# One decoder layer on one core: first layer norm folded into the second, router taken apart, all stages placed anew

## The chip, the cores and the metric

One Trainium2 chip, of which one core is used. Everything is in 32-bit floats. The metric is the time of one execution on the device in microseconds (us); lower is better. TensorE is PE in the profile, VectorE is DVE, ScalarE is ACT, GpSimd is POOL and SyncE, which here only issues DMAs, is SP.

## The reference, cut to what is computed

A decoder layer over 128 sequences of 64 tokens with 128 features each, three blocks with a layer norm (no gain, no bias) behind each sum:

```python
x = layernorm(x + mamba(x))                     # LN1
x = layernorm(x + retention(x, ctx, ctx))       # LN2
x = layernorm(x + moe(x))                       # LN3

# mamba: 256 inner channels, 16 states, 4 taps
x_b, z = split(x @ W_in)
xc = silu(conv4(x_b) + conv_b)
delta_raw, B, C = split(xc @ W_xproj)           # 8, 16 and 16 columns
delta = softplus(delta_raw @ W_dt + b_dt)
h = exp(delta * A) * h + delta * B * xc         # over time, for each channel and state
y = (sum_s h * C + D * xc) * silu(z)
out = y @ W_out

# retention: q of x, k and v of ctx, positions rotated (xpos), no softmax
out = ((q @ k.T) * decay_mask) @ v              # within a sequence

# moe: 16 experts of 64, the 2 best by logits, plus one shared expert of 128
logits = x @ router_w.T + bias
two scores of the best two, softmax over the two -> combine (tokens x 16)
out = sum_e combine_e * (silu(x @ gate_e) * (x @ up_e)) @ down_e + shared(x)
```

## The kernel before, in words

**Tiling.** The 8192 tokens are cut into 17 chunks: 15 of 512 tokens (8 whole sequences) with one of 256 at either end. A chunk is two halves ("subs") of 256 tokens; the scan of a sub takes 8 steps, each for `PAIR` = 2 of the 16 states. That makes 256 steps in the run, and a chunk of 512 tokens has 16. Channels lie on the 128 partitions, 256 inner channels as two halves side by side, so that each scan is 128 x 512.

**One step.** ACT makes the decays of the step by four exps of 128 x 252 (`decay`, L680, seven buffers). DVE multiplies delta*xc with the broadcast B of two states (`drive_bank` from `dx_bank` and `bc_all`, L720, two drives) and runs two scans (`state`, L822). POOL multiplies the states with C (`read`, L873, 128 x 1024, two buffers for states and reads). PE adds the results up over the states by eight transposes into `y_bank` (L287). B and C reach all partitions by DMA: SP stores `proj` to DRAM and loads it back in broadcast, four states a load (`bc_all`, L982, three buffers).

**The rest of a chunk** is done between the steps of others: input transpose, convolution (its first half as four matmuls on PE, its second half as three multiply-adds `conv` on DVE, L690), `xc` (ACT, L636 and L642), `proj`, `delta`; `y_gated` (DVE, L730), its transpose, the output projection `out_mm`; LN1; retention (`k_rot`, `q_rot` and their kin on POOL, L889 to L906); LN2; the router (DVE, L785 to L815, with an exp of ACT, L669, in the middle); then nine tiles of the FFN: a gate matmul, `silu` (ACT, L656), an up matmul, their product (DVE, L837; called `hid` for the shared expert and `gu` for the eight pairs of experts), the product with the experts' weights of the tokens (POOL `hid`, L916) and the down matmul. The weights of the tokens are broadcast by DMA too: `comb` is transposed (`combT`), stored (L1000) and loaded row by row (`comb_all`, L1009, three buffers).

**Layer norms.** All weights that feed a norm are centred once at the start (L742 to L758), so that the mean is zero and only a variance is wanted. A norm is: ACT squares four blocks of 128 x 128 with their sums (`square`, L522 to L528), POOL forms `var_eps` (L848) and `rstd` by a power (L852), ACT multiplies each block with it (`normalise`, L530 to L534). For LN1 PE then transposes the normalised rows `x1` and ACT copies the result as `x1T`.

**What sets the order of the work.** Each engine runs one program written out by a loop over `slot`, two slots a step, in which an `if` for each stage asks `chunk_at(slot, where, last)` whether this is the stage's slot; `where` is its place relative to the chunk, `last` that of the last chunk. Within a slot the order is that of the code. On DVE an even slot holds the two drives, an odd one the two scans, and everything else stands ahead of both or behind both. The nine tiles of the FFN have the places `FFN_AT`, and the exps of a sub are spread over seven slots (`decays_at`). Engines meet by semaphores; each waits in its own order, so whatever stands behind a waiting instruction waits too. Three PSUM banks are shared by all the matmuls that are not sums over a chunk: `take` hands out the one whose `slot` is lowest. The places around the change, as the code has them:

```python
EXP_AT = [10, 27]
FFN_AT = [69, 70, 72, 76, 78, 84, 88, 90, 91]
LAST_FFN_AT = [67, 68, 69, 71, 71, 74, 75, 77, 78]
if k % 2 == 0 and 0 <= (j := k // 2) < STEPS:       # two drives
if k % 2 == 1 and 0 <= (j := k // 2) < STEPS:       # two scans
```

## Time and profile before

| | |
|---|---|
| median of 3 runs | 1212.84 us (1212.56 to 1213.9) |
| profiled execution | 1216.39 us, its span 1214.6 us |
| mean granted clock of PE | 0.967 |
| first drive | 29.85 us |
| end of the last scan | 1137.6 us |
| DMA | 194.55 MB, 160 GB/s |

The span is cut in three: a head of 30 us until DVE begins the scans, 1108 us of steps, and a tail of 77 us in which the retention of the last chunk and the FFN of the last two are finished. The page gives for each engine its busy time; the windows view gives it for a stretch; the timeline lists instructions with their start, their duration and, in brackets, how long the engine had been idle and what released it. An instruction's duration overlaps with the next one's start where the two are independent, so a cost is read from start to start. In this profile the scans are called TENSOR_TENSOR_SCAN; in the lists of orders below they are SCALAR_TENSOR_TENSOR `state<-decay,drive_bank`.

### The profile page before, as it was taken

The page shows a single profiled execution, that of the slowest core. Times are in us where ns is not written, and L with a number is a line of the kernel's source. Part 1 is how long each engine was busy: PE and PEld are TensorE (multiplying, and loading weights), DVE is VectorE, ACT ScalarE, POOL GpSimd, SP SyncE. Part 2 cuts the span into 40 slices and gives each one's busy share as a digit, 9 for nine tenths or more (in the row PEclk, how much of TensorE's full clock was granted, in tenths as well). Part 3 has the DMA queues.
Part 4 walks back from the last instruction along what each step waited for, and adds up shares of the span by engine and source line. Part 5 has one row for each costly group of instructions (what it writes and reads, how often), then busy time and mean ns, then how long its engine had stood idle before and what let it go on. Part 6 is the DMA issues. An engine that isn't in the chain of part 4 may idle for free.

```text
span 1214.6 us, 18948 instructions
## 1 busy us (share of the span) xinstructions
PE 1080.0 (89%) x6049; PEld 766.0 (63%) x6049; DVE 1093.3 (90%) x1598; ACT 997.8 (82%) x2288; POOL 989.8 (81%) x623
## 2 busy tenths in 40 slices
PE   5677888989999898999989898998989899988897
PEld 2455666666666766666666666666666667666565
DVE  2899999999999999999999999999999999999523
ACT  5677888989888898988889898988889898888343
POOL 0587797979988897998888799888979888898844
PEclk9687999999999999999999999999999999999999
DMA  6344454545464454546455444645444465454221
GB/s 181 141 164 154 142 174 150 187 141 182 158 202 158 159 183 143 188 150 209 150 169 173 159 173 153 206 160 173 159 172 161 157 204 165 159 179 158 70 80 58
DMA packets 84116, 194.55 MB, mean 160 GB/s; under 512 B 17288, under 2 KB 47936, under 8 KB 67632
## 3 DMA queue, kind: packets, MB, share of 16 engines
q1 hardware_dynamic: 84016, 193.33, 47.3%
q8 instruction: 48, 0.79, 0.3%
q14 instruction: 52, 0.43, 0.1%
HBM read 179.14 MB, written 5.77 MB: 152 GB/s over the span
## 4 chain that ended last, share of the span: by engine, by line
ACT 34%; DVE 26%; PE 24%; issue 11%; POOL 3%; DMA 0%; SPq 0%; DVEq 0%; POOLq 0%; ACTq 0%
ACT decay L680 15%; PE bank L283 14%; DVE state L822 14%; DVE drive_bank L720 6%; PE y_bank L287 6%; ACT L680 4%; ACT silu L656 2%; PE down_bank L283 2%; PE bank L287 2%; ACT L636 1%; ACT L648 1%; ACT L656 1%; POOL hid L916 1%; ACT x_rows L526 1%; POOL read L873 1%
## 5 line engine op out<-in xcount | busy, mean ns | idle before, releaser
L873 POOL TENSOR_TENSOR read<-state,bc_all 128x1024 f32<-128x1024 f32 x256 | 605.4, 2365 | 162.4 <-DVE state L822 139.0
L822 DVE TENSOR_TENSOR_SCAN state<-decay,drive_bank 128x512 f32<-128x512 f32 x512 | 593.9, 1200 | 0.0
L680 ACT ACTIVATE decay<-delta,a_neg 128x252 f32<-128x252 f32 x1024 | 420.4, 494 | 0.8
L720 DVE TENSOR_TENSOR drive_bank<-dx_bank,bc_all 128x512 f32<-128x512 f32 x512 | 327.3, 685 | 0.3 <-DVE state L822 0.3
L287 PE MATMUL y_bank<-ident,read 128*128 128x128 f32 x2048 | 285.7, 287 | 40.4 <-POOL read L873 40.3
L287 PEld LDWEIGHTS y_bank<-ident,read 128*128 128x128 f32 x2048 | 246.2, 148 | 90.6 <-POOL read L873 57.6
L916 POOL TENSOR_TENSOR hid<-gu,comb_all 128x512 f32<-128x512 f32 (+1 forms) x136 | 165.0, 1213 | 20.1 <-DVE gu L837 16.6
L283 PE MATMUL down_bank<-down_w,hid 128*128 128x128 f32 x1024 | 140.9, 280 | 15.1 <-POOL hid L916 12.6
L656 ACT ACTIVATE silu<-bank 128x512 f32<-128x512 f32 (+1 forms) x153 | 87.3, 571 | 81.4 <-PE bank L283 79.6
L283 PEld LDWEIGHTS down_bank<-down_w,hid 128*128 128x128 f32 x1024 | 127.0, 191 | 38.0 <-POOL hid L916 28.6
L837 DVE TENSOR_TENSOR gu<-silu,bank 128x512 f32<-128x512 f32 (+1 forms) x136 | 86.8, 638 | 56.7 <-PE bank L283 30.0
L283 PE MATMUL bank<-x2T,gate_w 128*128 128x512 f32 (+1 forms) x272 | 132.9, 570 | 1.6 <-DVE conv L690 0.7
L283 PE MATMUL bank<-x2T,up_w 128*128 128x512 f32 (+1 forms) x272 | 132.7, 569 | 0.3 <-ACT silu L656 0.2
L283 PEld LDWEIGHTS bank<-x2T,up_w 128*128 128x128 f32 x272 | 51.2, 190 | 60.2 <-issue 52.8
L680 ACT ACT_TABLE_LOAD x63 | 80.8, 1283 | 1.1
L283 PE MATMUL bank<-xT,w_tap 128*128 128x512 f32 (+7 forms) x136 | 59.4, 582 | 0.0
L533 ACT ACTIVATE x_rows<-bank,rstd 128x128 f32<-128x128 f32 x128 | 36.9, 375 | 26.7 <-POOL rstd L852 26.7
L656 ACT ACT_TABLE_LOAD x45 | 57.7, 1283 | 0.8
L883 POOL TENSOR_TENSOR dx<-xc,delta 128x512 f32<-128x512 f32 x32 | 40.9, 1278 | 18.5 <-ACT delta L664 18.5
L852 POOL TENSOR_TENSOR rstd<-var_eps,minus_half 128x4 f32<-128x4 f32 (+1 forms) x51 | 49.7, 974 | 4.3
L283 PE MATMUL bank<-x2T,shared_w 128*128 128x512 f32 (+1 forms) x68 | 37.2, 638 | 16.9 <-ACT gate_z L648 11.4
L283 PEld LDWEIGHTS bank<-x2T,gate_w 128*128 128x128 f32 x272 | 42.8, 191 | 11.7 <-issue 8.0
(126 smaller groups left out, 1496.3 us busy)
## 6 DMA issues: line engine op xcount, KB each, us to landing
bc_all<-bc_dram SPq DMA_DIRECT2D x128, 1024.0 KB, 4.9
comb_all<-comb_dram SPq DMA_DIRECT2D x240, 128.0 KB, 4.5
x_in<-in_x_dram SPq DMA_DIRECT2D x15, 256.0 KB, 6.0
ctx_in<-in_ctx_dram SPq DMA_DIRECT2D x15, 256.0 KB, 5.2
k_pair<-k_pair SPq DMA_DIRECT2D x30, 128.0 KB, 2.1
q_pair<-q_pair SPq DMA_DIRECT2D x30, 128.0 KB, 2.0
out_dram<-y_out SPq DMA_DIRECT2D x15, 256.0 KB, 5.6
comb_all<-comb_dram SPq DMA_DIRECT2D x32, 64.0 KB, 2.7
```

The source lines that it names most:

```text
L283: return e.matmul(out, lhsT, rhs, start=start, stop=stop, skip_group_check=True)
L287: return e.matmul(out, in_, identity[0:n, 0:n], is_transpose=True, start=start, stop=stop, skip_group_check=True)
L533: done = e.activation(out[:, q, :], blocks(bank)[:, q, :], ACT.Copy, scale=rstd[i][:, q:q + 1])
L656: e.activation(silu[total % 2][:, 0:width(c)], bank_of["gate", c, index][:, 0:width(c)], ACT.Silu, scale=1.0).then_inc(S["silu"], 1)
L680: done = e.activation(seqs(decay_t[j % DECAYS][:, i, h, :])[:, :, 1:T], seqs(delta[c % 2][:, h, sub * SUB:(sub + 1) * SUB])[:, :, 1:T], AC ...
L720: e.tensor_tensor(drive_bank[:, n, :, :], dx_bank[:, :, :], bc_all[group % BC_BUFS][:, 0, PAIR * i + n, :].unsqueeze(1).to_broadcast([P, H ...
L822: e.tensor_tensor_scan(one(state_t[j % STATE_BUFS], n), one(decay_t[j % DECAYS], n), one(drive_bank, n), 0.0, ALU.mult, ALU.add).then_inc( ...
L837: e.tensor_tensor(target[:, 0:width(c)], silu[total % 2][:, 0:width(c)], bank_of["up", c, index][:, 0:width(c)], ALU.mult).then_inc(S["gu" ...
L852: e.tensor_tensor(rstd[i][:, 0:n], var_eps[i][:, 0:n], minus_half[:, 0:n], ALU.pow).then_inc(RSTD[i], 1)
L873: e.tensor_tensor(read_t[j % READS][:, :, :, :], state_t[j % STATE_BUFS][:, :, :, :], bc_all[group % BC_BUFS][:, 1, PAIR * i:PAIR * (i + 1 ...
L883: e.tensor_tensor(dx[sub][:, :, :], xc[c % 2][:, :, cols], delta[c % 2][:, :, cols], ALU.mult).then_inc(S["dx"], 1)
L916: e.tensor_tensor(hid[index % 3][:, 0:width(c)], gu[index % 2][:, 0:width(c)], comb_all[use % COMBS][:, 0:width(c)], ALU.mult).then_inc(S[ ...
```

## The change

**LN1 is folded into LN2.** Everything between LN1 and LN2 is linear in x1 (q is, the retention is, the sum is), so the scale of LN1 is a common factor of each token that LN2 takes out again; only the epsilon of LN2 has to be multiplied by LN1's variance (plus its epsilon) instead. `out_mm` now makes x1 directly in transposed form and without its scale, by three matmuls of up to 512 columns. The first, with `center`, stands ahead of the wait for y. ACT copies it as `x1T` and squares it into `r1_sq`; PE sums the squares over the features against a column of epsilons (`r1_var_mm`), ACT copies the 128 x 4 result, and POOL adds it in LN2's `var_eps`. Gone are LN1's squares and normalisation on ACT, its `var_eps` and `rstd` on POOL and its transposes on PE.

```diff
-                if (c := chunk_at(slot, 36, 33)) is not None:
-                    bank = take(("out", c), slot, 4.5)
+                for c in due(tick, "out_mm"):
+                    bank = take(("out", c), tick, 3)
+                    w.wait_ge(S["centered"], 1)
+                    mm(bank.t[:, 0:width(c)], center[:, :], xT[c % 3][:, 0:width(c)], stop=False)
                     w.wait_ge(S["yT"], subs_after(c))
-                    w.wait_ge(S["centered"], 1)
-                    for q in range(blocks_of(c)):
-                        cols = slice(q * P, (q + 1) * P)
-                        mm(bank.t[:, cols], xT[c % 3][:, cols], center[:, :], stop=False)
-                        for h in range(HALVES):
-                            done = mm(bank.t[:, cols], y_gatedT[:, h, cols], w_out[:, h, :], start=False,
-                                      stop=h == HALVES - 1)
+                    for h in range(HALVES):
+                        done = mm(bank.t[:, 0:width(c)], w_out[:, h, :], y_gatedT[:, h, 0:width(c)], start=False,
+                                  stop=h == HALVES - 1)
...
+                for c in due(tick, "r1_var_mm"):
...
+                    for q in range(blocks_of(c)):
+                        done = mm(bank.t[:, 2 * q:2 * q + 2], r1_sq[:, q * P:(q + 1) * P], eps_col[:, :])
...
-                    square(bank_of["out", c][:, :], x1, LN1, c)
-                if (c := chunk_at(slot, 38, 35)) is not None:
-                    normalise(bank_of["out", c][:, :], x1, LN1, c)
...
+                    copy(x1T[:, 0:width(c)], bank_of["out", c][:, 0:width(c)]).then_inc(S["x1T"], 1)
+                    w.wait_ge(S["r1_var_mm"], at(c - 1))
+                    e.activation(r1_sq[:, 0:width(c)], bank_of["out", c][:, 0:width(c)], ACT.Square, scale=D ** -0.5).then_inc(
+                        S["r1_sq"], 1)
...
+                if i == LN2:
+                    w.wait_ge(S["r1_var"], at(c))
+                    e.tensor_tensor(var_eps[i][:, 0:n], squares[i][:, 0:n], r1_var[:, 0:n], ALU.add).then_inc(VAR_EPS[i], 1)
```

**The router** has 17 operations for 19: the softmax over two is made by a tanh in place of exp, sum, reciprocal and product, the two scores are `0.5*tanh + 0.5` and `-0.5*tanh + 0.5`, and the two weighted ranks are one product of 128 x 128. Each operation has its own place.

**The grid.** A step has four ticks in place of two slots, on DVE one for each drive and scan, so that something may stand between any two. All places are a table of (place, place in the last chunk) in ticks, read by `due(tick, name)`; gate and up matmuls, silu, product, POOL's product, down matmul and comb load have a list of their own each, and every one of a chunk's 16 decays a tick.

```diff
+TICKS, SUM_AFTER = 4, 2
+SUB_TICKS = TICKS * SUB_STEPS
...
+AT = {
...
+    "top_tanh": [(131, 119)],
...
+    "k_rot": [(73, 88)],
...
+    "q_rot": [(86, 67)],
...
+    "silu": [
+        (139, 136), (140, 139), (144, 139), (152, 159), (157, 175), (167, 192), (177, 213), (177, 226), (178, 228)],
+    "gu": [
+        (142, 144), (144, 144), (149, 149), (157, 162), (160, 176), (171, 191), (179, 191), (184, 226), (188, 232)],
...
+    "route": [
+        (127, 108), (130, 109), (131, 110), (132, 111), (133, 112), (133, 113), (134, 114), (134, 115), (134, 116),
+        (134, 117), (134, 118), (134, 119), (134, 120), (135, 120), (135, 122), (136, 122), (136, 123)],
+}
+EXP_AT = [-9, -8, -2, -2, -2, 1, 4, 16, 22, 24, 26, 33, 36, 37, 38, 52]
...
+                j, part = divmod(tick, TICKS)
+                if 0 <= j < STEPS and part < PAIR:
...
+                    e.tensor_tensor(drive_bank[:, part, :, :], dx_bank[:, :, :],
...
+                if 0 <= j < STEPS and part >= PAIR:
+                    n = part - PAIR
...
+                for c, op in due(tick, "route"):
                     n = blocks_of(c)
...
+                    elif op == 12:
+                        done = e.tensor_tensor(soft[:, 0, 0:n], top[:, 0, 0:n], top[:, 1, 0:n], ALU.subtract)
+                    elif op in (13, 14):
+                        w.wait_ge(S["top_tanh"], at(c))
+                        done = e.tensor_scalar(soft[:, op - 11, 0:n], soft[:, 1, 0:n], 0.5 if op == 13 else -0.5, 0.5, ALU.mult, ALU.add)
+                    elif op == 15:
+                        w.wait_ge(S["combT_mm"], at(c - 1))
+                        done = e.tensor_tensor(rank[:, :, 0:n, :], comb[:, 0:2, 0:n, :],
+                                               soft[:, 2:4, 0:n].unsqueeze(3).to_broadcast([P, 2, n, EXPERTS]), ALU.mult)
+                    else:
+                        done = e.tensor_tensor(comb[:, 2, 0:n, :], rank[:, 0, 0:n, :], rank[:, 1, 0:n, :], ALU.add)
...
-                if slot % GROUP == 0 and 0 <= (group := slot // GROUP + 2) < ALL_SUBS * GROUPS:
+                if tick % (GROUP_STEPS * TICKS) == 0 and 0 <= (group := tick // (GROUP_STEPS * TICKS) + 2) < ALL_SUBS * GROUPS:
```

In the last chunk, the head and the tail all places are new too. In the head ACT's copies of the transposed weights (`w_qkv`, `shared_w`, `w_router`) stood behind the exps of decay 3 to 6, 16 instructions, and now stand behind decay 3's four.

**The order on DVE at a chunk's router.** This is the second router of the run. Before:

```order
L730 TENSOR_TENSOR y_gated<-gate_z,y_bank 128x512 [waits s_gate_z,s_y]
L785 TENSOR_TENSOR logits<-bank1,router_bias 128x64 [waits s_router_mm]
L771 TENSOR_REDUCE top<-logits 128x4 [waits s_comb,s_router]
L773 TENSOR_TENSOR rank<-logits,top 128x64 [waits s_router]
L775 TENSOR_TENSOR rank<-rank,expert_back 128x64 [waits s_router]
L777 TENSOR_REDUCE top_at<-rank 128x4 [waits s_router]
L779 TENSOR_TENSOR comb<-expert_back,top_at 128x64 [waits s_router]
L690 SCALAR_TENSOR_TENSOR masked<-comb,logits 128x64 [waits s_router]
L771 TENSOR_REDUCE top<-masked 128x4 [waits s_router]
```

and in the changed kernel:

```order
L799 SCALAR_TENSOR_TENSOR state1<-decay4,drive_bank 128x512 [waits s_drive]
L848 TENSOR_TENSOR logits<-bank0,router_bias 128x64 [waits s_comb,s_router_mm]
L791 TENSOR_TENSOR drive_bank<-dx_bank,bc_all2 128x512 [waits s_bc_load2,s_dx_bank,s_state]
L791 TENSOR_TENSOR drive_bank<-dx_bank,bc_all2 128x512 [waits s_state]
L799 SCALAR_TENSOR_TENSOR state0<-decay5,drive_bank 128x512 [waits s_read,s_decay,s_drive]
L852 TENSOR_REDUCE top<-logits 128x4 [waits s_router]
L799 SCALAR_TENSOR_TENSOR state0<-decay5,drive_bank 128x512 [waits s_drive]
L855 TENSOR_TENSOR rank<-logits,top 128x64 [waits s_router]
L791 TENSOR_TENSOR drive_bank<-dx_bank,bc_all2 128x512 [waits s_state]
L857 TENSOR_TENSOR rank<-rank,expert_back 128x64 [waits s_router]
L791 TENSOR_TENSOR drive_bank<-dx_bank,bc_all2 128x512 [waits s_state]
L806 TENSOR_TENSOR y_gated<-gate_z,y_bank 128x512 [waits s_gate_z,s_y]
```

The router was one block between a drive pair's `y_gated` and the scans. Now its first operations stand one by one behind a drive or a scan and start a step earlier. The further ones: two behind `y_gated`, seven behind the next scan, two behind the other scan, two behind the next drive.

**The order on ACT at the second half of `xc`**, in the middle of a chunk's FFN. Before:

```order
L520 ACTIVATE dx_bank<-dx1 128x512 [waits s_drive,s_dx]
L636 ACT_TABLE_LOAD [waits s_y]
L636 ACTIVATE xc_0<-bank0,conv_b 128x512 [waits s_tap_mm]
L642 ACTIVATE xc_0<-conv 128x512 [waits s_conv_tap]
L656 ACTIVATE silu1<-bank2 128x512 [waits s_gu,s_gate_mm]
L680 ACT_TABLE_LOAD
L680 ACTIVATE decay2<-delta1,a_neg 128x4x63 [waits s_state]
```

and in the changed kernel:

```order
L594 ACTIVATE dx_bank<-dx1 128x512 [waits s_drive,s_dx]
L709 ACT_TABLE_LOAD [waits s_y]
L709 ACTIVATE xc_0<-bank0,conv_b 128x512 [waits s_tap_mm]
L725 ACTIVATE silu1<-bank2 128x512 [waits s_gu,s_gate_mm]
L715 ACTIVATE xc_0<-conv 128x512 [waits s_conv_tap]
L749 ACT_TABLE_LOAD
L749 ACTIVATE decay2<-delta1,a_neg 128x4x63 [waits s_state]
```

The silu of an FFN tile (`silu1`) now stands between the two halves of `xc` instead of behind both. On DVE the product `gu` that reads it stood behind the scans of the step and ahead of the next two drives; it now stands between these two drives.

**The order on SP**, the DMA issues around a router's result. Before:

```order
L982 DMA bc_all1<-bc_dram1 128x2048 [waits s_read]
L1017 DMA ctx_in1<-in_ctx_1024_dram 128x4x128 [waits s_ctxT_mm]
L1000 DMA comb_dram1<-combT 16x512 [waits s_combT]
L982 DMA bc_all2<-bc_dram1 128x2048 [waits s_read]
L1009 DMA comb_all2<-comb_dram1 64x512 [waits s_hid,s_comb_store1]
L1009 DMA comb_all2<-comb_dram1 64x512
L1009 DMA comb_all0<-comb_dram1 64x512 [waits s_hid]
```

and in the changed kernel:

```order
L1040 DMA k_pair<-k_pair 64x512
L1033 DMA bc_all1<-bc_dram1 128x2048 [waits s_read]
L1051 DMA comb_dram1<-combT 16x512 [waits s_combT]
L1059 DMA comb_all2<-comb_dram1 64x512 [waits s_hid,s_comb_store1]
L1059 DMA comb_all2<-comb_dram1 64x512
L1059 DMA comb_all0<-comb_dram1 64x512 [waits s_hid]
L1059 DMA comb_all0<-comb_dram1 64x512
L1033 DMA bc_all2<-bc_dram1 128x2048 [waits s_read]
```

The broadcast load of `bc_all2` stood between the store of `combT` and the first loads of `comb_all`; now it stands behind the store and four of these loads.

## Rows read from the trace of the kernel before

**Rows 1.** The page's section 1: busy time, share of the span, instructions of each engine
```profile
PE 1080.0 (89%) x6049; PEld 766.0 (63%) x6049; DVE 1093.3 (90%) x1598; ACT 997.8 (82%) x2288; POOL 989.8 (81%) x623
```

**Rows 2.** Windows, chunk by chunk: length, busy time and count per engine, clock, DMA
```profile
443.33:514.50 71.17, 66.37 (x375) 47.18 (x374) 67.64 (x99) 61.67 (x142) 61.51 (x38) 0.98 0.49 168
514.50:584.12 69.62, 64.93 (x375) 45.43 (x374) 67.42 (x98) 61.66 (x142) 61.55 (x38) 1.00 0.52 172
...
sum 352.17, PE 328.49 PEld 232.30 DVE 337.74 ACT 308.33 POOL 307.67; mean PE 65.70 PEld 46.46 DVE 67.55 ACT 61.67 POOL 61.53
```

**Rows 3.** Timeline of DVE, one router block: start, duration, operation, [idle before]
```profile
544.82 0.22 DVE L785 TENSOR_TENSOR logits<-bank,router_bias 128x64 f32<-128x64 f32 x1
545.08 0.22 DVE L771 TENSOR_REDUCE top<-logits 128x4 f32<-128x64 f32 x1
...
548.44 0.17 DVE L804 TENSOR_SCALAR soft<-soft 128x4 f32<-128x4 f32 x1 [0.27 <-ACT soft L669]
...
549.45 0.23 DVE L815 TENSOR_TENSOR comb<-rank 128x64 f32<-128x64 f32 x1
549.59 2.32 DVE L822 TENSOR_TENSOR_SCAN state<-decay,drive_bank 128x512 f32<-128x512 f32 x2
```

**Rows 4.** Timeline of DVE, the steps behind that block
```profile
551.83 1.27 DVE L720 TENSOR_TENSOR drive_bank<-dx_bank,bc_all 128x512 f32<-128x512 f32 x2
553.01 2.32 DVE L822 TENSOR_TENSOR_SCAN state<-decay,drive_bank 128x512 f32<-128x512 f32 x2
555.25 1.27 DVE L720 TENSOR_TENSOR drive_bank<-dx_bank,bc_all 128x512 f32<-128x512 f32 x2
...
567.59 1.27 DVE L720 TENSOR_TENSOR drive_bank<-dx_bank,bc_all 128x512 f32<-128x512 f32 x2
```

**Rows 5.** Waits of DVE over the whole run: us in total, times, longest
```profile
DVE gu L837 <- ACT silu L656: 25.5, 23, 1.8
...
DVE hid L837 <- issue: 2.5, 13, 0.2
```

**Rows 6.** Timeline of DVE at the longer silu wait
```profile
578.30 0.69 DVE L837 TENSOR_TENSOR gu<-silu,bank 128x512 f32<-128x512 f32 x1 [1.15 <-ACT silu L656]
```

**Rows 7.** Timeline of ACT ahead of that wait
```profile
577.16 0.62 ACT L642 ACTIVATE xc<-conv 128x512 f32<-128x512 f32 x1
577.68 0.59 ACT L656 ACTIVATE silu<-bank 128x512 f32<-128x512 f32 x1
```

**Rows 8.** Windows of 2 us where the clock falls (columns as in rows 2)
```profile
452.00:454.00 2.00, 2.00 (x12) 2.00 (x11) 2.00 (x3) 1.28 (x9) 0.85 (x1) 0.50 0.95 264
```

**Rows 9.** Timeline of DVE behind that stretch
```profile
457.52 0.69 DVE L837 TENSOR_TENSOR gu<-silu,bank 128x512 f32<-128x512 f32 x1 [1.02 <-ACT silu L656]
```

**Rows 10.** Group of ACT: count | busy us, mean ns | idle before
```profile
L533 ACT ACTIVATE x_rows<-bank,rstd 128x128 f32<-128x128 f32 x128 | 36.9, 375 | 26.7 <-POOL rstd L852 26.7
```

**Rows 11.** Group of POOL, columns as in rows 10
```profile
L852 POOL TENSOR_TENSOR rstd<-var_eps,minus_half 128x4 f32<-128x4 f32 (+1 forms) x51 | 49.7, 974 | 4.3
```

**Rows 12.** Timeline of DVE in the head
```profile
39.07 0.29 DVE L751 TENSOR_REDUCE row_sum<-w_qkv 128x1 f32<-128x128 f32 x1 [4.51 <-ACT shared_w L520]
```

**Rows 13.** Timeline of ACT in the head
```profile
31.85 6.44 ACT L680 ACTIVATE decay<-delta,a_neg 128x252 f32<-128x252 f32 x16
...
38.56 0.47 ACT L520 ACTIVATE shared_w<-bank 128x384 f32<-128x384 f32 x1
```

**Rows 14.** Timeline of PE in the head
```profile
34.33 0.28 PE L287 MATMUL bank<-ident,router_rows 16*128 16x16 f32 x1
```

**Rows 15.** Timeline of ACT in the tail
```profile
1160.59 0.28 ACT L526 ACTIVATE x_rows<-bank 128x128 f32<-128x128 f32 x1 [0.20 <-PE bank L283]
...
1164.12 0.38 ACT L520 ACTIVATE x1T<-bank 128x256 f32<-128x256 f32 x1 [0.31 <-PE bank L287]
```

**Rows 16.** Timeline of SP's DMA issues
```profile
554.37 0.32 SPq L982 DMA_DIRECT2D bc_all<-bc_dram  x1
```

**Rows 17.** The page's section 6: DMA issues, count, KB each, us to landing
```profile
bc_all<-bc_dram SPq DMA_DIRECT2D x128, 1024.0 KB, 4.9
```

More of the change, by code:

```diff
@@ new lines, in decoder_layer @@
+        DUE = {name: {} for name in AT}
+        for name, places in AT.items():
+            for n, (normal, last) in enumerate(places):
+                due_of(name, n, normal, last)
+        EXP_DUE = {}
+        for j in range(STEPS):
+            half, n = divmod(j, SUB_STEPS)
+            virtual, sub = divmod(half + 1, SUBS)
+            step = SUB_STEPS * sub + n
+            place = SUB_TICKS * (SUBS * virtual - 1) + (EXP_AT[step] if virtual < CHUNKS - 1 else LAST_EXP_AT[step])
+            EXP_DUE.setdefault(place, []).append(j)
@@ L267, in decoder_layer, with due @@
+        ticks = [tick for places in (*DUE.values(), EXP_DUE) for tick in places]
+        FIRST_TICK, LAST_TICK = min(ticks), max(*ticks, TICKS * (STEPS + SUM_AFTER)) + 1
+        def due(tick, name):
+            return DUE[name].get(tick, ())
         block = ctx.enter_context(nc.Block())
@@ L301, in _ @@
                     bank.free = (S["xT"], at(c))
-                if (c := chunk_at(slot, -19, -18)) is not None:
-                    bank = take(("xb", c, 0), slot, 1.5)
+                for c in due(tick, "tap_mm"):
+                    bank = take(("xb", c, 0), tick, 3)
                     w.wait_ge(S["xT"], at(c))
@@ L364, in _ @@
                     bank.free = (S["ctxT"], at(c))
-                if (c := chunk_at(slot, 35, 35)) is not None:
-                    bank = take(("k", c), slot, 1)
+                for c in due(tick, "k_mm"):
+                    bank = take(("k", c), tick, 2)
                     w.wait_ge(S["ctxT"], at(c))
@@ L370, in _ @@
                     bank.free = (S["k_copy"], at(c))
-                if (c := chunk_at(slot, 36, 35)) is not None:
-                    bank = take(("v", c), slot, 1)
+                for c in due(tick, "v_mm"):
+                    bank = take(("v", c), tick, 2)
                     w.wait_ge(S["ctxT"], at(c))
@@ L413, in _ @@
+                for c in due(tick, "q_mm"):
+                    bank = take(("q", c), tick, 2)
                     w.wait_ge(S["x1T"], at(c))
@@ L443, in _ @@
                     bank.free = (S["x2T"], at(c))
-                if (c := chunk_at(slot, 63, 56)) is not None:
-                    bank = take(("router", c), slot, 1.5)
+                for c in due(tick, "router_mm"):
+                    bank = take(("router", c), tick, 3)
                     w.wait_ge(S["x2T"], at(c))
@@ L536, in _ @@
             w.wait_ge(S["first_consts"], 16 * 6)
-            for slot in range(FIRST, LAST):
-                if (c := chunk_at(slot, -21, -23)) is not None:
+            for tick in range(FIRST_TICK, LAST_TICK):
+                for c in due(tick, "xT"):
                     w.wait_ge(S["xT_mm"], at(c))
@@ L657, in _ @@
                                  scale=1.0).then_inc(S["silu"], 1)
-                if (c := chunk_at(slot, -9, -9)) is not None:
+                for c in due(tick, "delta"):
                     for h in range(HALVES):
@@ L828, in _ @@
+                    done.then_inc(S["comb" if op == 16 else "router"], 1)
+                for c, index in due(tick, "gu"):
                     total = TILES * c + index
@@ L890, in _ @@
                                     ALU.mult).then_inc(S["k_rot"], 1)
-                if (c := chunk_at(slot, 41, 43)) is not None:
+                for c in due(tick, "k"):
                     w.wait_ge(S["k_rot"], at(c))
@@ L899, in _ @@
                                     ALU.mult).then_inc(S["q_rot"], 1)
-                if (c := chunk_at(slot, 44, 36)) is not None:
+                for c in due(tick, "q"):
                     w.wait_ge(S["q_rot"], at(c))
@@ L984, in _ @@
                                     BC_LOAD[group % BC_BUFS], 16)
-                if (c := chunk_at(slot, 29, 38)) is not None:
+                for c in due(tick, "k_swap"):
                     w.wait_ge(S["k_copy"], at(c))
```

569 lines of the change are left out of this document (288 added, 281 removed).

## The prediction

> **What bounds the kernel now.** I read three views in this order: the busy line of the page, the windows chunk by chunk, and DVE's timeline inside one chunk. The busy line puts DVE and PE side by side, 1093.3 and 1080.0 us [rows 1], so it does not name the bound. The windows do [rows 2]: from one router block to the next, a chunk of 512 tokens takes 71.17 or 69.62 us, 70.43 in the mean of five (352.17 / 5), and DVE is busy for 67.55 of it. ACT has 61.67 and POOL 61.53. PE shows 65.70, but its records overlap and their ends are modelled, so I take it as having a few us of room. DVE is the bound, and what it does not work is waits of its own. Its timeline shows the price of one step [rows 4]: two drives 1.18 us (551.83 to 553.01) and two scans 2.24 (to 555.25), 3.42 together, 16 times a chunk = 54.7 us, which the change leaves alone. Some 15.7 us a chunk are router, `gu` and `hid` products, gates, taps and waits. There the change acts.
>
> **Term 1, the router.** Before, 19 small DVE operations stand in one block behind `y_gated`: 544.82 to 549.59 [rows 3] = 4.77 us, among them 0.27 us of waiting for ACT's exp. Neighbours that depend on each other start 0.26 us apart (544.82, 545.08) though one lasts 0.22. A follower that depends on nothing in the block starts earlier: the last comb starts at 549.45 and the scan behind it at 549.59, so this comb costs 0.14. After, 17 operations are spread over ten ticks. Eight small ones have a drive, scan or gate ahead and can take the 0.14 price (counting the 128x128 product at 0.2, my estimate by its size between the 0.23 of 128x64 and the 0.69 of 128x512 [rows 6]), the other nine follow one another at 0.26 or a little less: 7 x 0.14 + 0.2 + 9 x 0.25 = 3.43. The exp wait goes too, since a whole scan stands between the subtraction and the first use of ACT's tanh. Saving 4.77 - 3.43 = 1.34 us, at least 4.77 - 17 x 0.256 = 0.42 if place gives nothing, at most 4.77 - 17 x 0.14 = 2.4. I take 1.34 because both prices are rows of this very block. 14 routers lie in the pipeline: **-18.8 us** (5.9 to 34). The Trainium skill (Perfetto Trace Analysis, "Optimizing Scalar/DVE Operations") gives each DVE instruction on SBUF a fixed overhead of about 60 ns, counts the second half of its profiled time as covered by the next one, and advises fewer, larger operations. By it a small operation has one price wherever it stands, only the two that are left out and the exp wait count, and the sum would be rival A's. The trace does not agree: its price is 0.14 or 0.26 in one block, by what the operation has ahead of it.
>
> **Term 2, DVE's waits for silu.** DVE waits 25.5 us in 23 places for ACT's silu [rows 5]. 13 of them are 1.15 us, one a chunk [rows 6]: ACT, with no pause, copies xc's second half at 577.16 and only then does the silu at 577.68 [rows 7]. After, silu stands ahead of that copy (0.5 us earlier) and `gu` stands behind one more drive (0.6 later): 1.1 of 1.15 should go. 13 x 1.1 = **-14.3 us**, between 0 (ACT is later for another reason) and -15. Eight more are 1.02 us [rows 9] (13 x 1.15 + 8 x 1.02 = 23.1 of the 25.5; the other two lie at the run's ends). They follow a stretch in which PE's granted clock is 0.50 [rows 8], so that the gate matmul, and with it the silu, is late. Nothing in the change reaches this directly: 0 taken, -8.2 if the places happen to cover it. The 0.19 waits ahead of `hid` (2.5 us in 13 [rows 5]) and the one wide pair of taps that is taken apart are under 0.2 us a chunk each: 0 taken, -2.5 at most.
>
> **Term 3, the folded layer norm.** For each chunk ACT loses four squares with their accumulator reads and four normalising copies, and gains one 512-wide square (like a 0.59 silu [rows 7]) and a tiny copy. Whole-run, half of x_rows' 36.9 us of normalising [rows 10] goes, and half of its squares with it. POOL loses one of three rstd, 974 ns each [rows 11], and the `var_eps` before it. PE swaps twelve narrow matmuls for three wide ones, drops four transposes and adds four of two columns, about even. None of the three engines bounds a chunk [rows 2], so in the pipeline I cost this at nothing. DVE's cover is what hides it: if DVE were gone, ACT's 61.7 would be next, 6 us below what I forecast for a chunk. On POOL a read may now stand behind k_rot or q_rot, which were behind reads before; the scan two steps later waits for it, so up to one 2.4 us product fits without a DVE wait.
>
> **Term 4, the head.** DVE stands 4.51 us for ACT's copy of the shared weights [rows 12], because ACT does 16 decay pieces from 31.85 ahead of it and reaches the copy at 38.56 [rows 13]. PE has the transposed weights ready at 34.61 (34.33 + 0.28) [rows 14]. After, only four pieces are ahead (1.6 us), so that PE's transposes set the copy. The wait shrinks to some 0.3 us: **-4.2 us**, between 0 (the decays put off are then missed by a scan) and -4.5.
>
> **Term 5, the tail.** Behind the last scan ACT's x_rows square at 1160.59 leads by rstd, normalise and PE's transposes to the x1T copy at 1164.12 [rows 15]; after, this is one copy: **-3.5 us**. Bounds: 0, since the last chunk's FFN queues behind the one before it on PE, and -10 with the new places.
>
> **The sum.** -18.8 - 14.3 - 4.2 - 3.5 = -40.8. The profiled execution took 1216.39 us (span 1214.6), 3.55 over the median of 1212.84. 1216.39 - 40.8 = 1175.6; less 3.55, **1172.0 us**. A chunk should take 70.43 - 1.34 - 1.0 = 68.1 us.
>
> **Rivals.**
> A, *place gives nothing*: small operations cost 0.256 everywhere. Router -5.9 in place of -18.8: 1184.9 us. For it: 16 of the 17 still carry a wait on the one before. Against: the 0.14 row.
> B, *the waits stay*: ACT's and PE's order moves the silu wait elsewhere and the tail gives nothing, -23.0 left: 1189.8 us. For it: all stages were moved at once on three shared PSUM banks. Against: ACT has 2 us a chunk more room.
> C, *all waits go*: 8.2 + 2.5 + 0.7 more, and 6.5 more in the tail, -58.7: 1154.1 us. For it: a grid twice as fine can reach them; against: the clock's falls are not the grid's.
> D, *slower, by the bc load*: before, SP issues bc_all at 554.37 ahead of the comb loads [rows 16], it takes 4.9 us to land [rows 17], and the drive at 567.59 [rows 4] is the first to need it: 8.3 us of slack. After, this load stands behind the comb store, which waits for the router's result, and four comb loads; I estimate 5.5 us later (the landing of the store, the four issues, and a comb that is ready a tick later), 2.8 of slack. Each us beyond costs 14 us in the run, every drive and scan being queued behind. It decides from 2.9 us (40.8 / 14) over the slack on; at 4 us, -40.8 + 56 = +15.2: 1228.0 us. Against: comb would have to be over 5.7 us later than I estimate, and DVE's router starts five ticks earlier.
> E, *nothing net*: smaller new waits of some 2.9 us a chunk of any engine eat the gain: about 1213.
>
> **How the numbers follow.** Forecast 0.49, A 0.14, B 0.14, C 0.12, D 0.08, E 0.03. About 0.2%, 2.4 us, is what a measurement here can tell from no change. Faster: the first four, 0.89; same 0.03; slower 0.08. The forecast's own range is 1165 to 1180. The whole range takes in C, A and B with a few us: 1153 to 1195, and leaves out D, E and what lies below C.
>
> **What would show it.** Router: between two steps that hold a router operation, 0.14 us more than 3.42 for each single one; a chunk at 68.1. Silu: no 1.15 row ahead of `gu`, but 1.02 rows still behind stretches at clock 0.50. Head: DVE's wait for shared_w near 0.3. POOL and ACT about 60 and 59 us a chunk. The prediction is wrong if a chunk stays above 70 us or if DVE waits for a DMA of bc_all, for a read, or for decays each chunk.

## The result, and the profile after

The changed kernel takes 1254.85 us (median of 4 runs, 1254.38 to 1255.52) against 1212.71 us: a ratio of 1.035, 95% interval 1.033 to 1.036. It is 42 us slower where 41 us less was forecast.

The page of the changed kernel, its busy line, which answers to [rows 1]:

```profile
span 1252.6 us, 18269 instructions
...
PE 1072.2 (86%) x5831; PEld 752.8 (60%) x5831; DVE 1160.4 (93%) x1564; ACT 975.3 (78%) x2128; POOL 972.0 (78%) x590
```

PE, ACT and POOL have less to do, as meant. DVE has 34 instructions fewer and is busy 67.1 us longer. Its idle time (span less busy) fell from 121.3 to 92.2 us. So the span's 38.0 us are +67.1 of busy DVE and -29.1 of waits: in their sum the waits went as forecast or a little better, and the loss lies inside instructions that count as busy.

The windows chunk by chunk, from router to router as in [rows 2]:

```profile
413.74:486.32 72.58, 65.01 (x362) 45.20 (x361) 71.86 (x96) 60.48 (x132) 60.47 (x35) 0.98 0.50 165
...
558.90:632.82 73.92, 64.69 (x363) 45.25 (x361) 71.99 (x96) 60.48 (x132) 60.43 (x35) 0.98 0.46 162
...
sum 365.72, PE 324.33 PEld 226.71 DVE 359.56 ACT 302.35 POOL 302.25; mean PE 64.87 PEld 45.34 DVE 71.91 ACT 60.47 POOL 60.45
```

A chunk takes 73.14 us (before 70.43, forecast 68.1), and DVE is busy for 71.91 of them (67.55). The groups of DVE (count | busy us, mean ns | idle before) say which instructions:

```profile
L868 DVE TENSOR_SCALAR soft<-soft 128x4 f32<-128x4 f32 (+1 forms) x34 | 38.3, 1128 | 1.5 <-ACT soft L738 1.0
...
L857 DVE TENSOR_TENSOR rank<-rank,expert_back 128x64 f32<-128x64 f32 (+1 forms) x34 | 33.4, 983 | 0.7
L871 DVE TENSOR_TENSOR rank<-comb,soft 128x128 f32<-128x128 f32 (+1 forms) x17 | 30.2, 1776 | 0.1
...
L861 DVE TENSOR_TENSOR comb<-expert_back,top_at 128x64 f32<-128x64 f32 (+1 forms) x34 | 7.5, 221 | 1.2
L859 DVE TENSOR_REDUCE top_at<-rank 128x4 f32<-128x64 f32 (+1 forms) x34 | 7.1, 210 | 0.7
```

Three kinds of router operation are some four to seven times as long as work of their size; the others stay at 0.16 to 0.22 us. One chunk's timeline on DVE shows them one by one:

```profile
557.67 0.20 DVE L852 TENSOR_REDUCE top<-logits 128x4 f32<-128x64 f32 x1
...
559.62 1.88 DVE L857 TENSOR_TENSOR rank<-rank,expert_back 128x64 f32<-128x64 f32 x1
...
564.88 0.23 DVE L857 TENSOR_TENSOR rank<-rank,expert_back 128x64 f32<-128x64 f32 x1
...
566.87 2.55 DVE L868 TENSOR_SCALAR soft<-soft 128x4 f32<-128x4 f32 x2
...
569.93 1.90 DVE L871 TENSOR_TENSOR rank<-comb,soft 128x128 f32<-128x128 f32 x1
```

And the same stretch on POOL:

```profile
556.13 2.38 POOL L926 TENSOR_TENSOR read<-state,bc_all 128x1024 f32<-128x1024 f32 x1
559.07 2.35 POOL L926 TENSOR_TENSOR read<-state,bc_all 128x1024 f32<-128x1024 f32 x1 [0.55 <-DVE state L799]
...
567.03 2.36 POOL L926 TENSOR_TENSOR read<-state,bc_all 128x1024 f32<-128x1024 f32 x1 [4.24 <-DVE state L799]
569.34 2.34 POOL L941 TENSOR_TENSOR k_pair<-k_pair,xpos 128x1024 f32<-128x1024 f32 x1
```

Each long operation ends with a POOL instruction: 559.62 + 1.88 = 561.50 and the read ends at 561.42; 566.87 + 2.55 = 569.42 and the read ends at 569.39; 569.93 + 1.90 = 571.83 and k_rot ends at 571.68. The second `rank<-rank,expert_back`, of the same shape, runs at 564.88, when POOL is idle, in 0.23. What stands still all have two operands in SBUF (or are a tensor_scalar from SBUF to SBUF); the reduce at 557.67 has one and takes 0.20 in the middle of the read of 556.13. Drives, scans and gates have their second operand in PSUM (`dx_bank`, `drive_bank`, `y_bank`) and never show it.

The Trainium skill says it outright (SBUF — State Buffer, "Who interferes with whom"): a DVE instruction with two SBUF inputs contends with a GpSimd instruction that reads SBUF, whichever comes first holds the shared port for its whole length and the other fully blocks; a tensor_scalar can contend too, by a mode that takes both of DVE's ports, and a tensor_reduce never does. For these three the trace agrees, with 1.7, 2.2 and 1.6 us a chunk more than the same work takes in the run e1 below. The prediction should have weighed this page, and did not.

The hint had been in the trace of before: the first rank operation of the router took 0.33 us instead of 0.22, because it began 0.25 us before a read's end. The rest of the block ran while POOL did two operations of 128x4 (`var_eps`, `rstd`) and then, waiting for the scans behind the block, was idle.

### The profile page after: what moved, and what is told of

Its sections match the earlier page's. It is cut to its first block, busy times and chain, and to the rows that moved or that the text cites. A ratio compares the mean times of both kernels' runs of the same rounds, so it can differ in the third digit from the quotient of the medians.

```text
span 1252.6 us, 18269 instructions
## 1 busy us (share of the span) xinstructions
PE 1072.2 (86%) x5831; PEld 752.8 (60%) x5831; DVE 1160.4 (93%) x1564; ACT 975.3 (78%) x2128; POOL 972.0 (78%) x590
## 4 chain that ended last, share of the span: by engine, by line
PE 32%; POOL 17%; ACT 17%; DVE 16%; issue 16%; DMA 1%; SPq 1%; POOLq 0%; ACTq 0%; DVEq 0%
PE bank L361 18%; POOL read L926 11%; DVE state L799 7%; ACT decay L749 7%; PE y_bank L370 6%; PE down_bank L361 5%; POOL hid L967 3%; DVE drive_bank L791 3%; PE bank L370 3%; DVE rank L871 2%; ACT L749 2%; ACT L709 2%; ACT silu L725 2%; POOL ret L958 1%; POOL dx L935 1%
## 5 line engine op out<-in xcount | busy, mean ns | idle before, releaser
L799 DVE TENSOR_TENSOR_SCAN state<-decay,drive_bank 128x512 f32<-128x512 f32 x512 | 602.2, 1206 | 0.0
L791 DVE TENSOR_TENSOR drive_bank<-dx_bank,bc_all 128x512 f32<-128x512 f32 x512 | 336.6, 685 | 0.0
L370 PE MATMUL y_bank<-ident,read 128*128 128x128 f32 x2048 | 274.6, 280 | 45.2 <-POOL read L926 45.2
L370 PEld LDWEIGHTS y_bank<-ident,read 128*128 128x128 f32 x2048 | 238.3, 144 | 93.6 <-POOL read L926 54.9
L725 ACT ACTIVATE silu<-bank 128x512 f32<-128x512 f32 (+1 forms) x153 | 87.6, 574 | 96.6 <-PE bank L361 96.2
L361 PE MATMUL bank<-x2T,up_w 128*128 128x512 f32 (+1 forms) x272 | 133.7, 574 | 10.2 <-ACT proj L594 6.8
L361 PE MATMUL down_bank<-down_w,hid 128*128 128x128 f32 x1024 | 135.3, 277 | 0.7 <-POOL hid L967 0.7
L887 DVE TENSOR_TENSOR gu<-silu,bank 128x512 f32<-128x512 f32 (+1 forms) x136 | 88.2, 649 | 34.8 <-PE bank L361 20.7
L361 PEld LDWEIGHTS bank<-x2T,up_w 128*128 128x128 f32 x272 | 46.9, 190 | 52.6 <-issue 31.4
L935 POOL TENSOR_TENSOR dx<-xc,delta 128x512 f32<-128x512 f32 x32 | 41.0, 1281 | 18.8 <-ACT delta L733 18.8
L361 PE MATMUL bank<-xc,w_xproj 128*40 128x512 f32 (+1 forms) x68 | 34.4, 634 | 24.1 <-ACT xc L715 23.6
L594 ACT ACTIVATE combT<-bank 16x512 f32<-16x512 f32 (+1 forms) x17 | 9.5, 561 | 55.2 <-PE bank L370 55.2
L370 PE MATMUL bank<-ident,y_gated 128*128 128x128 f32 x128 | 22.4, 303 | 32.3 <-DVE y_gated L806 32.3
```

What stands on the lines that cost most here:

```text
L361: return e.matmul(out, lhsT, rhs, start=start, stop=stop, skip_group_check=True)
L370: return e.matmul(out, in_, identity[0:n, 0:n], is_transpose=True, start=start, stop=stop, skip_group_check=True)
L725: e.activation(silu[total % 2][:, 0:width(c)], bank_of["gate", c, index][:, 0:width(c)], ACT.Silu, scale=1.0).then_inc(S["silu"], 1)
L791: e.tensor_tensor(drive_bank[:, part, :, :], dx_bank[:, :, :], bc_all[group % BC_BUFS][:, 0, PAIR * i + part, :].unsqueeze(1).to_broadcast ...
L799: e.tensor_tensor_scan(one(state_t[j % STATE_BUFS], n), one(decay_t[j % DECAYS], n), one(drive_bank, n), 0.0, ALU.mult, ALU.add).then_inc( ...
L887: e.tensor_tensor(target[:, 0:width(c)], silu[total % 2][:, 0:width(c)], bank_of["up", c, index][:, 0:width(c)], ALU.mult).then_inc(S["gu" ...
```

## The experiments

Theory L: the lock just described. Rival P: small operations are dear on DVE behind large ones, or in their new forms. Rival W: waits in another place. In this table idle is span less busy of DVE, from each profiled run. The kernel before, run beside each group of experiments, gave 1214.5 us (e1 to e3), 1214.3 (e4 to e7) and 1215.9 (e8 to e11), so that 2 or 3 us between two groups mean nothing.

| run | time, us | span | DVE busy | DVE idle |
|---|---|---|---|---|
| before | 1212.7 | 1214.6 | 1093.3 | 121.3 |
| changed | 1254.9 | 1252.6 | 1160.4 | 92.2 |
| e1, router one block again | 1180.8 | 1179.0 | 1084.6 | 94.4 |
| e2, k_rot a step later | 1225.0 | 1223.3 | 1135.7 | 87.6 |
| e10, early rank product into the block | 1247.6 | 1245.4 | 1138.3 | 107.1 |
| e11, tensor_scalars into the block | 1267.1 | 1264.7 | 1161.9 | 102.8 |
| e4, e1 with three edits | 1180.4 | 1180.3 | 1083.2 | 97.1 |
| e5, e1 with a norm's work put back | 1192.5 | 1190.0 | 1084.1 | 105.9 |
| e7, e1 with all 17 in the block | 1206.0 | 1203.1 | 1087.8 | 115.3 |
| e8, e1 with the tanh early | 1175.1 | 1171.5 | 1084.3 | 87.2 |
| e9, e8 with operation 2 alone | 1174.4 | 1171.2 | 1082.9 | 88.3 |
| e3, before with POOL reading beside the router | 1236.3 | 1233.8 | 1116.2 | 117.6 |
| e3, before with memsets beside it | 1214.6 | 1212.4 | 1094.4 | 118.0 |
| e6, before with the router ahead of the drives | 1284.1 | 1281.8 | 1120.5 | 161.3 |

**e1: only the places of the router undone.** Of the changed kernel's table, 13 numbers:

```diff
-        (127, 108), (130, 109), (131, 110), (132, 111), (133, 112), (133, 113), (134, 114), (134, 115), (134, 116),
-        (134, 117), (134, 118), (134, 119), (134, 120), (135, 120), (135, 122), (136, 122), (136, 123)],
+        (127, 108), (130, 109), (134, 110), (134, 111), (134, 112), (134, 113), (134, 114), (134, 115), (134, 116),
+        (134, 117), (134, 118), (134, 119), (134, 120), (134, 120), (134, 122), (134, 122), (134, 123)],
```

> The changed kernel with operations 2 to 16 of the router together again at one place, between a step's two scans, where POOL has finished its read; operations 0 and 1, all other places, the folded norm and the 17 operations stay as changed. Theory L (a DVE operation that reads two SBUF operands, or a tensor_scalar in SBUF, stands still while POOL runs one that reads SBUF): no router operation over 0.4 us, DVE busy about 5 us a chunk less, 1254.9 - 14 x 5 = about 1185 us. Rival P (small operations are dear behind a drive or scan for a reason of DVE's own, or are dear because of the new forms, the 128x128 product and the tensor_scalars): the 128x128 product stays near 1.9 us and the tensor_scalars near 1.1, time above 1220. Rival W (other new waits are the loss): 1240 or more.

Measured 1180.81 us, 74.0 less than changed and 0.9725 (0.9711 to 0.974) of before. Groups of DVE in this run:

```profile
L857 DVE TENSOR_TENSOR rank<-rank,expert_back 128x64 f32<-128x64 f32 (+1 forms) x34 | 8.6, 252 | 1.2
...
L871 DVE TENSOR_TENSOR rank<-comb,soft 128x128 f32<-128x128 f32 (+1 forms) x17 | 5.9, 348 | 0.6
L868 DVE TENSOR_SCALAR soft<-soft 128x4 f32<-128x4 f32 (+1 forms) x34 | 5.8, 170 | 6.7 <-ACT soft L738 6.1
```

The same instructions, forms and operands, 75.8 us less busy. So new forms and other new waits are out as the cause, and the fold, the new places of everything else and the 17 operations together are a gain of 32 us (34 against the runs of before beside it). "No router operation over 0.4 us" holds in 16 of the 17 routers; in the last one, in the tail, two take 1.25 and 1.31 us beside POOL's `hid` products, as they do in the changed kernel. A chunk takes 68.29 us in this run (`logits` at 321.68 and 389.97), where the prediction had 68.1.

**e3: the lock brought into the kernel before.** In the program of POOL, behind the read of the router's step, where it had been idle for 5 us:

```diff
+                if (c := chunk_at(slot, 65, 56)) is not None:
+                    w.wait_ge(S["extra"], at(c - 1, 1, 2))
+                    e.tensor_tensor(extra[:, :], extra_in[:, :], extra_in[:, :], ALU.mult).then_inc(S["extra"], 1)
+                    w.wait_ge(S["extra"], at(c, 0, 2))
+                    e.tensor_tensor(extra[:, :], extra_in[:, :], extra_in[:, :], ALU.mult).then_inc(S["extra"], 1)
```

and in the second run `e.memset(extra[:, :], 1.0)` twice instead.

> The kernel before with two additional POOL multiplications of 128x512 (about 1.2 us each, SBUF to SBUF, result unused) in each chunk behind the read ahead of the router block, where POOL had been idle for 5 us. Theory L: they overlap with the router block and its two-operand operations wait for them; the block takes 1 to 2.4 us more, 14 x 1.7 = 24 us more, 1235 us (1225 to 1246), and some rank operations show 1 us or more. Rival P: POOL was idle, nothing changes, 1213 us.

> As the run with the additional multiplications, but with two memsets of 128x512 in their place, which read nothing. Theory L in the form that only POOL's reads of SBUF stand in the way of a second operand: no change for the rank operations; at most the four tiny tensor_scalar-like ones could meet them, 1213 us within 2. If POOL's work of any kind blocks DVE: as much more as with the multiplications, in proportion to the memsets' own time.

Measured 1236.29 us (ratio 1.018, 1.017 to 1.020) and 1214.58 (1.0005, 0.9996 to 1.0015; the runs of before beside them had 1214.46). With the multiplications DVE is busy for 22.9 us more than in before. Timeline of DVE with the multiplications, and of POOL:

```profile
551.57 0.97 DVE L777 TENSOR_TENSOR rank<-rank,expert_back 128x64 f32<-128x64 f32 x1
552.57 0.22 DVE L779 TENSOR_REDUCE top_at<-rank 128x4 f32<-128x64 f32 x1
552.83 0.83 DVE L781 TENSOR_TENSOR comb<-expert_back,top_at 128x64 f32<-128x64 f32 x1
```

```profile
551.41 1.04 POOL L882 TENSOR_TENSOR extra<-extra_in 128x512 f32<-128x512 f32 x1
552.53 1.04 POOL L884 TENSOR_TENSOR extra<-extra_in 128x512 f32<-128x512 f32 x1
```

The reduce between the two waits for nothing though POOL's second multiplication is under way; its two neighbours do. With the memsets, DVE and then POOL:

```profile
544.49 0.23 DVE L777 TENSOR_TENSOR rank<-rank,expert_back 128x64 f32<-128x64 f32 x1
...
546.03 0.23 DVE L777 TENSOR_TENSOR rank<-rank,expert_back 128x64 f32<-128x64 f32 x1
```

```profile
544.30 0.53 POOL L882 MEMSET extra<- 128x512 f32 x1
544.89 0.52 POOL L884 MEMSET extra<- 128x512 f32 x1
...
545.66 1.01 POOL L854 TENSOR_TENSOR rstd<-var_eps,minus_half 128x4 f32<-128x4 f32 x1
```

For the two-operand products only POOL's reads of SBUF stand in the way, as the page has it. That the memsets are half as long does not explain it: the product began inside one of them and lasted no longer. A tensor_scalar is another matter. In one router of this run, in the tail, one meets the second memset, and takes 0.58 us where it takes 0.17 alone:

```profile
1160.51 0.58 DVE L806 TENSOR_SCALAR soft<-soft 128x4 f32<-128x4 f32 x1 [1.25 <-ACT soft L671]
```

```profile
1160.55 0.52 POOL L884 MEMSET extra<- 128x512 f32 x1
```

Both end within 0.02 us of each other (1161.09 and 1161.07), so that an instruction of POOL which only writes can hold up a tensor_scalar. This is one case in one run.

**e2, e10, e11: one collision at a time.** Of the changed kernel, only: `k_rot` (73 to 77) with its sum `k` (77 to 81); or the places of operations 3 to 5 (132, 133, 133 to 134); or those of 13 and 14 (135 to 134).

> The changed kernel with one POOL operation moved: k_rot from behind the read of the router's step to behind the read of the next one (tick 73 to 77, its sum from 77 to 81). Theory L: the 128x128 product of the router, 1.9 us beside k_rot, falls to about 0.3, while the early rank product (1.88, beside a read) and the second tensor_scalar (2.4, beside a read) stay as they are: 14 x 1.6 = 22 us less, about 1232 us. Rival P: no operation changes, 1255 us.

> The changed kernel with the early rank product (operation 3) and the two behind it moved into the block between the two scans; the tensor_scalars and the 128x128 product stay where they are. Theory L: the product's 1.88 us fall to 0.23, 14 x 1.65 = 23 us less, less 0.1 us a chunk for the longer block: 1254.9 - 22 = about 1233 us; the other two long ones stay.

> The changed kernel with the two tensor_scalars moved from behind the second scan, where POOL's read starts, into the block ahead of it; the early rank product and the 128x128 product stay. Theory L: the second tensor_scalar's 2.4 us fall to 0.2, a tanh wait of 0.34 comes back: 14 x 1.85 = 26 us less, about 1229 us, if the 128x128 product stays beside k_rot; the early rank product stays at 1.88.

e2 gave 1225.0 us, 30 less, of which 24.7 are busy time: the product's mean fell from 1776 to 333 ns, the two other kinds kept 985 and 1128. That is as expected, and 8 us more, made up of 2.7 of busy time and 4.6 of shorter waits in the profiled spans.

e10 gave 1247.6, a miss in the time. The operation did what was said (mean 983 to 239 ns), DVE was busy for 22.1 us less, but waited 14.9 us more. Silu waits of `gu` doubled, from 10.2 to 20.5 us; why the silu is late there I have not followed up.

e11 gave 1267.1, a miss with the wrong sign, and the more telling for it. The tensor_scalars fell to 170 ns. Timeline of DVE, then of POOL:

```profile
574.43 2.09 DVE L870 TENSOR_TENSOR rank<-comb,soft 128x128 f32<-128x128 f32 x1
576.55 2.25 DVE L873 TENSOR_TENSOR comb<-rank 128x64 f32<-128x64 f32 x1
```

```profile
574.00 2.36 POOL L925 TENSOR_TENSOR read<-state,bc_all 128x1024 f32<-128x1024 f32 x1 [4.95 <-DVE state L798]
576.32 2.39 POOL L940 TENSOR_TENSOR k_pair<-k_pair,xpos 128x1024 f32<-128x1024 f32 x1
```

With the tensor_scalar gone, the 128x128 product meets the read it used to come behind, and the sum behind it, short until now, meets k_rot. A collision had held the next one off. Over the run the tensor_scalars gave back 32.5 us, while the sum took 30.3 more (3.8 to 34.1) and the product 2.6 more; in all, DVE's busy time rose by 1.5 us. The other 10.6 us are waits, 5.1 of them for the tanh, which the expectation had, and 3.6 for silu ahead of `gu`. Taking a collision away does not save its length; the whole row of two-operand work has to leave POOL's reads.

**e6: the old block in another place.** In the kernel before, the router's code moved ahead of that of the drives, the gating and the taps, nothing else.

> The kernel before with one edit: the router's first 13 operations stand ahead of the step's two drives instead of behind drives and y_gated, so that they begin as POOL's read begins. Theory L: the first rank operation waits for the read to end, 1.9 us, less the 0.27 us of waiting for exp that is now covered: 14 x 1.6 = 22 us more, 1236 us. Rival P: the order of drives and router makes no difference but the exp wait, 1209 to 1213 us.

Measured 1284.1 us (ratio 1.057, 1.055 to 1.058). The rank operation meets the read as said (timeline of DVE, and POOL's read of that step):

```profile
568.97 2.10 DVE L723 TENSOR_TENSOR rank<-logits,top 128x64 f32<-128x64 f32 x1
...
577.31 0.17 DVE L754 TENSOR_SCALAR soft<-soft 128x4 f32<-128x4 f32 x1 [1.93 <-ACT soft L669]
```

```profile
568.64 2.35 POOL L873 TENSOR_TENSOR read<-state,bc_all 128x1024 f32<-128x1024 f32 x1 [0.89 <-DVE state L822]
```

That is 27 us of busy time. The other 40 us were not in the expectation: DVE's wait for the exp grew from 5.3 to 30.2 us in all, that for the shared expert's silu from 4.3 to 25.2. ACT is in order, and its exp stands behind the `y_gatedT` copy (576.59, after 4.87 us of idleness), and that copy hangs on the gating, which the router now goes ahead of. PE's mean clock is lower too in this run, 0.926 against 0.967; what share of the 40 us that has is not shown.

**e5: what the fold is worth.** In the run e1, at the x1T copy:

```diff
+                    for q in range(blocks_of(c)):
+                        done = e.activation(extra[:, q, :], blocks(bank_of["out", c][:, :])[:, q, :], ACT.Square, scale=1.0,
+                                            accum_out=extra_sq[:, q:q + 1])
...
+                    for q in range(blocks_of(c)):
+                        done = e.activation(extra[:, q, :], blocks(bank_of["out", c][:, :])[:, q, :], ACT.Copy, scale=0.5)
```

and one power of 128 x 4 on POOL.

> The run with the router as one block, with the work of a first layer norm on ACT and POOL put back as dead work in each chunk, at the x1T copy: four squares with their sums, four scaled copies (about 2.2 us of ACT), and one rstd-like power on POOL (1 us). Theory of the prediction (the fold takes work from engines that DVE covers): 1181 us within 5, waits for silu may grow a little. Rival (ACT or POOL is so near the path that the fold itself carried the gain of this version): 14 x 2.2 = 31 us more, 1200 or above.

Measured 1192.48 us, 11.7 more than e1: more than nothing, less than the rival's 31. It is dead work: nothing waits for its results, so what the chain from squares to scaled rows cost before is not in it. ACT is busy 25.3 us longer and DVE waits 11.5 us longer, mostly for silu (6.4 to 14.1 us ahead of `gu`, 9.3 to 12.7 ahead of `hid`). DVE covers about half of ACT's work at that place.

**e4, e7, e8, e9: how the block is best laid.**

> The run with the router as one block between two scans, with three edits: the subtraction of the two best logits, and with it the tanh, moved ahead of the second one-hot (the block waited 0.34 us for tanh); operation 2 alone directly behind a second scan, where it asks before POOL's read does; the gating y_gated one tick later (it waited 0.41 us for y_bank in each chunk). Theory L: no long router operation, 0.34 + 0.41 + 0.11 = 0.86 us a chunk less, 1180.8 - 12 = about 1169 us. Rival P: operation 2 behind the scan is dear (1.9 us or so), and the time stays at 1181 or goes up.

> The run with the router as one block, with operations 0 and 1 in the block as well instead of alone behind scans. If a small operation costs 0.11 to 0.14 alone and 0.26 in a row, 14 x 2 x 0.13 = 3.6 us more, 1184.5 us; if place gives nothing, 1180.8 us.

e4 gave 1180.4, no gain. The two waits went (tanh 6.1 to 1.0 us, y_gated 10.0 to 4.0) and those for silu took their place (6.4 to 17.5). The later `y_gated` is what spoils it: e9, below, is e4 without that edit and takes 1174.4. PE waits 26.8 us for `y_gated` in e4 (3.9 in e1); that everything behind it then reaches ACT later is the likely way, which I have not traced. e7 gave 1206.0, 25 us more, not 3.6. Waits of PE in that run:

```profile
PE bank L360 <- DVE logits L847: 33.5, 15, 2.9
```

Operation 0 is what frees the shared PSUM bank of the router's matmuls. It now comes seven ticks later, and so PE's next user of the bank is late. DVE waits 20.0 us for the tanh (6.1 in e1); that the delay gets there by ACT's copies is argued, not traced. So this run does not measure the price of a place alone. That price is in the rows of e1: `logits` at 526.54 has the drive behind it at 526.66, so 0.12 us alone; in the block neighbours start 0.26 apart.

e8 and e9 then take only the edits that harm nobody: operation 12, the subtraction, behind operation 7 instead of 11, and in e9 also operation 2 at tick 131.

```diff
+FORM = [0, 1, 2, 3, 4, 5, 6, 7, 12, 8, 9, 10, 11, 13, 14, 15, 16]
...
-                    w.wait_ge(S["router"], at(c, 12, ROUTER))
+                    w.wait_ge(S["router"], at(c, 8, ROUTER))
```

> The run with the router as one block, with only the subtraction (and so ACT's tanh) moved ahead of the second one-hot. The block's 0.34 us wait for tanh goes: 14 x 0.34 = 4.8 us less than 1180.8, about 1176 us. If the silu waits that came up in the run with three edits come from this edit, 1180 or more.

> As the run with the early tanh, and operation 2 alone directly behind a step's second scan. It asks for its operands 0.1 us before POOL's read starts, so it stays at 0.2 us; the block is 0.12 us shorter: 14 x 0.12 = 1.7 us less, about 1174.5 us. If it loses the race to the read it takes 2 us and the run is 25 us slower.

Measured 1175.14 and 1174.40 us, ratios 0.9668 (0.9653 to 0.9682) and 0.9665 (0.9647 to 0.9684) of before. Both as expected; the 0.7 us between them are less than these runs can tell apart. Either beats both kernels.

## Why the prediction was wrong

**Term 1, the router, is the step that failed.** "Eight small ones have a drive, scan or gate ahead and can take the 0.14 price": of these, operations 0, 1 and 2 took 0.11 to 0.12 each, and the rows of 4 to 5 and 6 to 12 took 0.38 and 1.61 us, close to the 0.39 and 1.64 that 0.14 and 0.25 give. But operations 3 and 15 took 1.8 and 1.9, and 14, one of the nine, 2.3. The lock adds about 5.4 us a chunk (1.88 for 0.22, 2.55 for the 0.38 of e1, 1.90 for its 0.29), 76 us in 14 routers; forecast -15.0 of busy DVE (-18.8 less the exp wait) plus 76 is +61, measured +67.1. The other prices were sound: start to start the 17 operations took 8.7 us in this chunk, and less the 5.4 that is 3.3, an estimate, against the 3.43 forecast. No run has the router spread out and free of the lock; e1, with the block back, takes 4.2 us for all 17 against 4.77. The term's ends were too narrow as well. "At least 0.42 if place gives nothing" took the block's own rows as the worst case, and in those rows POOL was idle or at work on 128x4: a price is only good for the company in which it was measured.

**Term 2, silu, held in its sum, not in its parts.** All waits of `gu` for silu came to 10.2 us in 10 places, from 25.5 in 23 ([rows 5]): -15.3 against -14.3. But the wait at the second half of `xc` went in 8 chunks of 14, not in all; in the other six (the first at 232.50, the last at 1038.15) it is 1.17 to 1.18 us. Timeline of ACT at one of these six, which answers to [rows 7]:

```profile
597.03 0.69 ACT L709 ACTIVATE xc<-bank,conv_b 128x512 f32<-128x512 f32 x1
597.62 0.59 ACT L725 ACTIVATE silu<-bank 128x512 f32<-128x512 f32 x1
598.09 0.63 ACT L715 ACTIVATE xc<-conv 128x512 f32<-128x512 f32 x1
```

The silu leads as said, at a distance from the table load in front that is the same in chunks with the wait and without; DVE reaches `gu` 1.3 us after that table load begins in this chunk, and 2.5 us after it in the chunk before, where there is no wait. The six chunks with the wait are those of 73.9 to 74.1 us, the others that follow one another in the steady part take 72.6. What makes the two kinds differ stays open. What made up for the chunks with the wait are the eight waits of 1.02 us behind low clock [rows 9], for which nothing was taken: none is left, though the clock is still 0.98 in the mean of a chunk. That the sum came out is luck in this part, and in others: a wait that no term has, that of the gating for `y_bank`, came up. Waits of DVE (us in total, times, longest), before and then changed:

```profile
DVE y_gated L730 <- PE y_bank L287: 0.6, 1, 0.6
```

```profile
DVE y_gated L806 <- PE y_bank L370: 10.3, 15, 2.8
```

Against that, the waits of `gu` for PE fell from 30.0 to 20.7 us.

**Term 3, the fold, was costed at nothing and is worth more.** POOL and ACT fell to 60.45 and 60.47 us a chunk (60 and 59 forecast). With the lock away, its ACT and POOL work would cost 12 us (e5). "None of the three engines bounds a chunk" is true and does not make their work free: an in-order engine with 8 us to spare a chunk can be late at one place.

**Term 4, the head, held.** `row_sum` stands at 34.60 with no wait ([rows 12]: 39.07), and the scan behind it at 36.41 instead of 40.20: -3.8 against -4.2. The missing part is the lock again, 0.7 us in the 128x2 tensor_scalar between them, beside the read of 33.58 to 35.94 (0.17 us before):

```profile
35.10 0.86 DVE L830 TENSOR_SCALAR row_mean<-row_sum 128x2 f32<-128x2 f32 x1
```

**Term 5, the tail, held:** from the last scan's end to the end of the span 72.5 us against 77.0, -4.5, forecast -3.5. How much of it is the fold and how much the new places, no run separates.

**The rivals.** D was the slower one, by another mechanism: no wait of DVE for bc_all stands in the changed kernel's list of waits. What "would make the prediction wrong" named waits of DVE and a chunk above 70 us; the chunk was, the waits were not. No case had the busy time of DVE going up. With 34 instructions fewer and each priced by its own row, a rise could come from the new forms, which e1 rules out, or from something they share with another engine, and I had asked what the moved operations wait for, never what runs beside them.

## What to carry to other kernels

Before moving a DVE operation, note where its operands lie and what POOL does at the new place. With two SBUF operands, or a tensor_scalar in SBUF, it may wait out a whole POOL instruction that reads SBUF (one that only writes held up a tensor_scalar once), 2.4 us here for 0.2 of work, and the profile books this as busy time of the instruction, not as a wait: look for a group whose mean is many times that of its neighbours of equal size. Such work belongs in one row at a time when POOL has run dry, here between a step's two scans; reduces and operations with one side in PSUM showed no such delay anywhere in these runs.

## What the runs showed of the hardware that was not expected

An operation that stands right behind a scan can win against the read which the same scan releases: in the changed kernel operation 2 begins at 558.90 and the read at 559.07, and in e9 operation 2 has 0.20 us in the mean of 17 routers and 0.275 at most (the last router's; the last two stand behind no scan). A POOL power of 128 x 4 does not disturb, though its operands lie in SBUF; here the measurement goes against "for its whole length": `rstd` runs 1.01 us at 545.66 in the memset run while three two-operand operations of DVE at 545.77, 546.03 and 546.55 take 0.22 to 0.23. How long a small POOL instruction holds the port, no run here measures, nor what a large one with a single SBUF operand does; the spans on POOL are rough.
